# A gated expert block with a quantised feed-forward: the opening and the last expert step in another order on every engine

## The reference

```python
def _L0_xattn_ref(hidden_states, token_ids, Wg, Wu, Wd):     # Wg = Wu = Wd = ctx_2048, 4 experts of 512 x 512
    expert_ids = jnp.minimum(jnp.clip(token_ids, 0, 24999) // 6250, 3)
    for e in range(4):
        g = jax.nn.silu(jnp.einsum('bsd,fd->bsf', hidden_states, Wg[e]))
        u = jnp.einsum('bsd,fd->bsf', hidden_states, Wu[e])
        y = jnp.einsum('bsf,df->bsd', g * u, Wd[e])
        out = jnp.where((expert_ids == e)[..., None], y, out)
def _L0_ffn_ref(x, gate_w, up_w, down_w, ...):               # 512 -> 1536 -> 512, weights rounded to fp8
    gate = jax.nn.silu(_quantized_matmul(x, gate_w, gate_scale))
    up = _quantized_matmul(x, up_w, up_scale)
    return _quantized_matmul(gate * up, down_w, down_scale)
x = x + jnp.tanh(g_xattn[0]) * _L0_xattn_ref(_layernorm(x), itok, ctx_2048, ctx_2048, ctx_2048)
x = x + jnp.tanh(g_ffn[0]) * _L0_ffn_ref(_layernorm(x), gate_w, up_w, down_w, ...)
```

## Time and profile before

| | us |
|---|---|
| median of 3 runs | 406.75 |
| lowest, highest | 406.28, 407.37 |
| the profiled execution's own time | 406.11 |
| its span | 404.4 |
| PE busy | 379.4 (94%) |
| DVE, ACT, POOL busy | 219.1, 187.3, 161.2 |

### The profile page before, as it was taken

How to read it: one execution, slowest core, us unless ns; L and a number is a source line. 1 busy time by engine, 2 the same in 40 slices (tenths; PEclk the granted TensorE clock), 3 DMA queues, 4 the chain that set the end, 5 groups by cost and what they waited for, 6 DMA issues and landing times.

```text
span 404.4 us, 6038 instructions
## 1 busy us (share of the span) xinstructions
PE 379.4 (94%) x1912; PEld 183.2 (45%) x1912; DVE 219.1 (54%) x465; ACT 187.3 (46%) x294; POOL 161.2 (40%) x199
## 2 busy tenths in 40 slices
PE   2889799999999899999999999999999999999990
PEld 2445355545555444444444444444444444444440
DVE  5876888797867786787524222224222225222243
ACT  4777756787886536694432222222222222222220
POOL 2678989997989930411008100006200005300003
PEclk9999999999999999999999999999999999999997
DMA  7697783444445340670002000001100001100002
GB/s 259 167 343 196 138 193 113 68 117 80 105 105 117 94 104 2 151 165 25 0 2 78 28 0 0 2 0 53 52 0 0 0 0 40 66 0 2 0 0 104
DMA packets 40075, 29.99 MB, mean 74 GB/s; under 512 B 31192, under 2 KB 31216, under 8 KB 40048
## 3 DMA queue, kind: packets, MB, share of 16 engines
q1 hardware_dynamic: 37488, 21.26, 22.2%
q0 software_dynamic: 2560, 8.39, 6.1%
HBM read 18.11 MB, written 4.19 MB: 55 GB/s over the span
## 4 chain that ended last, share of the span: by engine, by line
PE 81%; DVE 8%; POOL 3%; issue 3%; ACT 2%; DMA 1%; DVEq 0%; POOLq 0%; ACTq 0%
PE bank L1415 41%; PE bank L1423 20%; PE bank L1314 9%; PE bank L1333 8%; PE bank L1262 2%; POOL xs L502 1%; DVE stats L978 1%; DMA xs<-in_x,order 1%; DVE row_hot L913 1%; ACT xn L676 1%; DVE xs L1243 1%; DVE hTl L995 1%; DVE X L1240 1%; DVE xs L1028 1%; ACT hTh L744 1%
## 5 line engine op out<-in xcount | busy, mean ns | idle before, releaser
L1415 PE MATMUL bank<-X,W 128*128 128x512 f16 (+1 forms) x768 | 173.3, 379 | 0.0
L1415 PEld LDWEIGHTS bank<-X,W 128*128 128x128 bf16 x768 | 75.0, 98 | 90.9 <-ACT late_norms L802 0.5
L1189 DVE SCALAR_TENSOR_TENSOR cs<-bank,up_mul,cs 128x512 f32<-128x512 f32 x48 | 36.0, 751 | 108.7 <-PE bank L1415 104.6
L1423 PE MATMUL bank<-W,cs 128*128 128x512 bf16 x376 | 88.7, 379 | 0.0
L776 ACT ACTIVATE cs<-bank,gate_mul 128x512 f32<-128x512 f32 x48 | 32.9, 686 | 80.0 <-PE bank L1415 80.0
L783 ACT ACTIVATE cs<-cs 128x512 f16<-128x512 f32 x47 | 29.5, 628 | 77.8 <-DVE cs L1189 77.6
L633 POOL TENSOR_TENSOR xs<-xs,X 128x512 f32<-128x512 f32 x12 | 15.3, 1274 | 125.2 <-DVE X L1240 124.9
L1423 PEld LDWEIGHTS bank<-W,cs 128*128 128x128 f16 x376 | 36.5, 98 | 43.7 <-DVE cs L1197 0.2
L1333 PE MATMUL bank<-M,X 128*128 (+1 forms) x228 | 52.3, 379 | 3.1 <-DVE X L999 2.1
L1197 DVE TENSOR_TENSOR cs<-cs 128x512 f16<-128x512 f32 x47 | 33.8, 719 | 31.5 <-ACT cs L783 31.5
L1314 PE MATMUL bank<-M,hTh 128*128 (+1 forms) x152 | 45.1, 378 | 3.2 <-DVE xs L1028 3.2
(11 more groups left out here) (164 smaller groups left out, 379.8 us busy)
## 6 DMA issues: line engine op xcount, KB each, us to landing
ws<-in_L_ffn_gate_w SPq DMA_DIRECT2D x12, 256.0 KB, 2.7
ws<-in_L_ffn_up_w SPq DMA_DIRECT2D x12, 256.0 KB, 2.7
ws<-in_L_ffn_down_w SPq DMA_DIRECT2D x12, 256.0 KB, 2.9
cs<-in_ctx SPq DMA_DIRECT2D x2, 1024.0 KB, 6.6
X<-in_ctx SPq DMA_DIRECT2D x2, 1024.0 KB, 6.9
xs<-in_x,order POOLq DMA_INDIRECT x16, 4.3
dsc<-in_L_ffn_down_scale SPq DMA_DIRECT2D x1, 256.0 KB, 7.0
X<-x2rows SPq DMA_TRANSPOSE x16, 3.1
```

Source lines behind the costliest of these rows:

```text
L1189: v.scalar_tensor_tensor(out=fuse[:, c % 2, :], in0=UP[c % 2][:], scalar=up_mul[:, c:c + 1], in1=sg[:, c % 2, :], op0=ALU.mult, op1=ALU.mu ...
L1415: ins = t_.matmul(dst[c % 2][:].rearrange("p (t i) -> p t i", t=TPG), w, x2_group(g, part, k), start=(k == 0 and part == 0), stop=(k == KC ...
L1423: ins = t_.matmul(ACC[t][:], fuse_part(g, c, part)[:, t * P:(t + 1) * P], W8[:, down_slab(c), :], start=(c == 0 and part == 0), stop=(c == ...
```

## The change

No product is added or left out. What moves:

- **Sort.** The last three of the sixteen `row_hot` blocks are made by POOL (`last_hot`), around its `tile_tok`.
- **Opening on PE.** z of step 0 is cut in two; after its sixth matmul PE turns x of tile 1 into a second bank (`XT` becomes two banks, 2 and 4) and sums the squares for the scales of experts 1 and 2. In steps 1 to 3 the next x is turned ahead of z, from step 4 on behind it as before. The 6 and 4 matmuls that only fill time (on `bank7`) are gone; the 16 ahead of the first turn stay. The three words of the expert walk are loaded before z of step 0. The f32 sum for expert 3 goes from step 1 to step 2.
- **ACT.** Expert 2's squares are cut in two halves; expert 3's squares go from step 0 to step 1; `expert_rows_high` of 1 stays in step 0, that of 2 and the rescaling go to step 2, that of 3 to the head of step 3, and expert 3's rescaling is dropped.
- **POOL.** `step_mask` becomes `mask_places`, `mask_starts`, `mask_last`, laid between the gathers and `ln_scalars`; `y_table` becomes one of 3 steps (experts 0 to 2) before step 0 and one of 16 steps in step 1; expert 3's low part leaves POOL; gathers 9 to 15 are issued later, in steps 0 and 2 to 4.
- **DVE.** `expert_scales(1)`, `step_hot` and the small tables stand elsewhere in step 0, the tables of all experts in step 2; `expert_low(1)` goes from step 0 to step 1; `expert_low(3)` is new on DVE, in step 3; `x1_low` is ahead of `product_h` in steps 0, 1, 3 and 4; `dsb` is made in the feed-forward's first group.
- **Slabs.** Steps with two slabs are 7, 9, 12, 14, 16 instead of 5, 8, 11, 14, 16; slab 0 is rounded at the head of POOL's step 2.
- **Last step.** `h_low(17)` and `add_expert(16)` stand ahead of the chain of small operations `ffn_norms`.

```diff
         def quantised(lo):
-            return 0 if lo < 2 or lo >= STEPS - 1 else 2 if lo in (5, 8, 11, 14, 16) else 1
+            return 0 if lo < 2 or lo >= STEPS - 1 else 2 if lo in (7, 9, 12, 14, 16) else 1
...
             def step(s, lo):                          # POOL
                 if lo >= X2_LAG:
                     x2_low(s - X2_LAG)
+                if lo == 2:
+                    round_slab(0, 0)
                 ln_scalars(s + STATS1_LEAD, lo % 2, 0 if lo + STATS1_LEAD < TILES else 1,
                            2 if lo >= STATS2_LAG else 1)
                 if lo == 0:
-                    y_table()
-                if lo < 2:
-                    expert_low(lo + 2)
-                slabs = slabs_of(s, lo)
+                    gather(9, gathered[5])
+                    expert_low(2)
+                if lo == 1:
+                    y_table(1, E, slice(E - 1, STEPS))
+                slabs = slabs_of(s, lo) if lo != 2 else []
...
             def step(s, lo):                          # ACT
+                if lo < 2 or lo in (3, 4):
+                    x_high(s + 1)
                 if lo < 2:
+                    normalise(s + 2)
+                if lo == 2:
+                    expert_rows_high(2)
+                    normalise(4)
+                    expert_rows_scaled(2)
+                if lo == 3:
+                    expert_rows_high(3)
+                silu(s, lo)
...
             def product_z(s, lo, matrices, operands): # PE
+                pe.wait_ge(m_ready, matrices)
                 pe.wait_ge(xlo_done, min(s + 1, TILES))
                 for n, (lhs, rhs) in enumerate(operands):
+                    if lo == 0 and n == 6:
+                        turn_x(1)
+                        pe.wait_ge(ssq_done, 4)
+                        t_.matmul(SMALL[:, M_SUM + 1:M_SUM + E - 1], ones32[:], part_ssq[:, 1:E - 1], ...)
...
             def step(s, lo):                          # PE
-                product_z(s, lo, z_next[0])
-                if lo < TILES - 1:
-                    pe.wait_ge(xn_done, s + 2)
-                    transpose4(XT, xn, xT_done)
-                if lo == 0:
-                    for i in range(WORDS):
-                        load_word(t_, words, i)
-                    for i in range(6):
-                        t_.matmul(bank[7][:], row_hot[:, 0, :], row_hot[:, 0:KC, :]...)
+                if 1 <= lo < E:
+                    turn_x(s + 1)
+                product_z(s, lo, *z_next[0])
+                if E <= lo < TILES - 1:
+                    turn_x(s + 1)
...
             def step(s, lo):                          # DVE
+                if lo == 3:
+                    expert_low(3)
+                    h_low(s - 1, lo - 1)
+                    add_expert(1)
                 product_h(s, lo)
-                if lo == STEPS - 1:
-                    ffn_norms(SMALL, 0, 2)
...
+                if lo >= 1 and lo != 3:
+                    h_low(s - 1, lo - 1)
+                if lo == STEPS - 1:
+                    norms_in()
+                    add_expert(s - 2)
+                    ffn_norms(0, 2)
```

More of the change, by code:

```diff
@@ L216, in build @@
         order_done = sem("order_done")
-        gathered = [sem(f"gathered{i}") for i in range(7)]
+        gathered = [sem(f"gathered{i}") for i in range(8)]
         mask_done = sem("mask_done")
@@ L514, in ln_scalars, with mask_places @@
                                 ALU.mult).then_inc(ln_done, 1)
[L516 to L528, removed]
             starts = [base[:, e * TILES:e * TILES + 1] for e in range(1, E)]
-            def step_mask():
+            def mask_places():
                 pool.wait_ge(e_of_done, 1)
@@ L570, in expert_low @@
                                     ALU.subtract).then_inc(mlow_pool, 1)
-            step_mask()
-            for t in range(10, 12):
-                gather(t, gathered[5])
+            gather(0, gathered[0])
+            gather(1, gathered[1])
+            gather(2, gathered[1])
+            mask_places()
+            ln_scalars(0, 0, 0, 1)
+            gather(3, gathered[2])
+            mask_starts()
+            ln_scalars(1, 1, 0, 1)
+            gather(4, gathered[3])
+            ln_scalars(2, 2, 0, 1)
+            gather(5, gathered[3])
+            gather(6, gathered[4])
+            ln_scalars(3, 3, 0, 1)
+            gather(7, gathered[4])
+            mask_last()
+            y_table(0, E - 1, slice(0, E - 1))
+            gather(8, gathered[5])
             def round_slab(n, slot):
@@ L680, in x_high @@
                 act.wait_ge(xT_done, tile + 1)
[L681 removed]
+                a.activation(x2_part(tile, 0), XT[tile % 2][:].rearrange("p (k i) -> p k i", k=KC),
                              ACT.Copy).then_inc(xhi_done, 1)
@@ L1126, in step @@
                     aggregate(3, 3, 0, 1)
+                    load_word(v, words, 0)
+                if lo == 1:
+                    expert_low(1)
+                if lo == 2:
+                    round_stats(1, 1)
+                    expert_scales(E - 1, E)
+                    expert_y_scales(1, E - 1, E)
+                    add_expert(0)
+                if lo == 3:
+                    expert_low(3)
+                    h_low(s - 1, lo - 1)
+                    add_expert(1)
+                product_h(s, lo)
@@ L1392, in norms @@
                 ins.then_inc(norm_done, 1)
+            for i in range(WORDS):
+                load_word(t_, words, i)
             z_next = [z_operands(0, 0)]
```

259 lines of the change are left out of this document (147 added, 112 removed).

## The result

| | median us | lowest, highest | executions |
|---|---|---|---|
| before | 407.16 | 406.04, 408.50 | 20 |
| changed | 404.54 | 403.31, 410.45 | 20 |

The ratio is 0.9947 with an interval of 0.9933 to 0.9960, which is 2.2 us; the medians differ by 2.6. I had forecast 4.0 (402.7). So it is faster, by roughly half to two thirds of the forecast; 404.54 lies inside my range (400.9 to 404.9), near its upper end. The profiled execution took 404.58, with a span of 402.8. The two highest times are of disturbed executions and are not in the ratio.

The account below looks back on a forecast made before the run. PE was taken as the bound, busy 379.4 of 404.4 us, with waits and filling left in the opening. Opening 3.6, middle 0 and last step 0.4 sum to 4.0 us, giving a median of 402.7, range 400.9 to 404.9.

Parts of the forecast that it names:

- Opening: PE from the first z to y2: less waiting and filling, gain 3.6 us (4.0 less 0.4), ends 2.2 and 4.3.
- z0 at 18.76: First z on PE: three sort blocks moved to POOL bring its start from 19.32 to 18.76, 0.56 us earlier.
- z2 at 27.5: z of step 2 on PE starts 2.6 us earlier, with `x1_low(2)` ending at 26.9.
- Rest: Small leftovers: walk loads covered by the 1.50 us wait before z0, `dsb` costs nothing, transposes and slab 4's load earlier.
- The collision that I had counted: Opening: DVE's `expert_low(3)` blocks POOL for 2.2 us; with 4.50 taken off it, POOL nets +2.3.
- The 0.4 that I had set aside for steps 4 to 6: Steps 4 to 6: DVE stays some 0.5 us behind, z6 waits for `x1_low(6)`, losing another 0.3 to 0.6.
- Rival A: Opening: DVE's three long expert operations delay PE and meet POOL; opening gives 2.2, end 0, so 404.5 us; chance 0.11.
- Middle: Steps after the opening: POOL's nearly full row keeps up with PE, priced at 0, from -0.4 to +0.4 us.
- Last step: y17 starts 0.86 us earlier, 0.45 is given back before y18; net +0.4, from -0.1 to +0.86.
- Rival C: Opening: the clock falls to 1.2 GHz in PE's waits, one step at that level costs 6.2 us, so 408.9; chance 0.03.
- B: POOL's 21st slab still ends at 138.4, PE waits before y18, all but some 0.5 given back, 406.2 us; chance 0.07.
- D: Sort: POOL's blocks cost 1.1 each or more, sort 0.5 later, 403.8 us; chance 0.77 together with the forecast.

Follow-up runs that it names:

- e3: Changed kernel with all 16 `row_hot` blocks on DVE and none on POOL: 404.99 us.
- e10: Changed kernel with DVE's load of the first walk word put ahead of the scales of experts 1 and 2: 404.07 us.
- e8: Changed kernel with expert 3's low part back on POOL and its rescaling back on ACT, as before: 406.73 us.
- e13: Changed kernel with, in step 10 only, DVE's add of step 8 ahead of that step's statistics: 403.30 us.
- e6: Changed kernel with the old slab counts and slab 4's load issued ahead of the last expert's transposes: 404.37 us.
- e2: Changed kernel with the old slab counts (two in steps 5, 8, 11, 14, 16): 409.80 us.
- e4: Changed kernel with the last step's old order on DVE, small norm chain ahead of `h_low(17)` and `add_expert(16)`: 404.20 us.
- e14: Changed kernel plus early word load, 6 fillings before z0, early slab 4 load, step 8's add first in step 10, add of 17 ahead of feed-forward scales: 402.49.

## Why the prediction was right in direction and wrong in size

- **Opening, forecast 3.6, measured 2.67 (z5).** The order of events was right, and y1's wait of 2.47 is gone as forecast. Two terms failed.
  - *z0 at 18.76, measured 19.29.* I took 0.56 for the sort and carried all of it to z0. `order` gained 0.37, and z0 was 0.03 to 0.2 earlier, since an idle of 0.36 is new ahead of DVE's preparation. From z0 to z5 are 30.2 us in seven traces with z0 between 19.17 and 19.31, so these 0.53 arrive at z5 in full. e3 shows that three blocks on POOL gave their 0.5 all the same: without them z0 is at 19.72.
  - *z2 at 27.5, measured 28.59.* I laid the order down by durations alone and left out the walk's word that DVE loads ahead of `product_h(0)`, priced under "Rest" as covered, which was true of PE's loads and not of DVE's. It stands as 0.76 of idle DVE:

```profile
25.45 0.75 DVE L1151 SCALAR_TENSOR_TENSOR h<-bank,h_scale,silu_z 128x512 f32<-128x512 f32 x1 [0.76 <-issue]
```

  e10 shows 0.96 between z1 and z2, of which 0.38 is left at z5.
  - y2 was late by 1.31; 0.53 and 0.38 of it are these two. For the other 0.4 DVE's row is the place, since it works without a pause from 37.15 to the end of `product_h(3)` at 46.36, for which PE waits 0.60. The collision that I had counted, DVE's `expert_low(3)` over POOL's table, costs DVE nothing (2.50, where `expert_low(1)` takes 2.48 before; POOL's table took 1.30 and 1.11 where e8 has 0.29 and 0.24, and PE doesn't wait for it). The one that I hadn't counted goes the other way. Under POOL's `expert_low(2)`, from 36.63 on, DVE's tables of step 2 took 0.57 and 1.19, and `w_big` 0.79; before they took 0.23, 0.21 and 0.43, together 1.7 less. That this makes the 0.4 is read from the trace and no run tests it. First the changed kernel, then before:

```profile
38.91 1.19 DVE L1063 TENSOR_TENSOR step_sel<-step_hot,h_scale 128x64 f32<-128x64 f32 x1
...
36.63 4.51 POOL L583 TENSOR_TENSOR W<-X,W 128x512 f16<-128x512 f32 x4 [1.63 <-ACT X L704]
...
34.01 0.21 DVE L1013 TENSOR_TENSOR step_sel<-step_hot,h_scale 128x64 f32<-128x64 f32 x1
```

  - The 0.4 that I had set aside for steps 4 to 6 was not needed: from y2 to z5 are 2.59 us before and after. That is luck: 1.31 less 0.4 are the 0.9 that the opening missed.
- **Rival A (DVE's debt) gives the right number for other reasons.** Its 404.5 is the measured median, and its 2.2 for the opening is near. But its three long pieces on DVE were no longer than before (`expert_scales(1)` 1.33, the low parts 2.47 and 2.50), and e8 shows that the alternative to `expert_low(3)` on DVE costs 2.2.
- **Middle, forecast 0, measured -0.76** (2.67 at z5, 1.91 at z18). It is one wait of 0.96 that comes or not by chance; without it the middle gains 0.2, and in e13's trace it takes 79.55 where before takes 79.89. My bounds of 0.4 had no room for a collision on the path. POOL's first rounding came at 45.11, not at 43.8, and its 21st slab ended at 136.5. The counts of slabs don't matter there (e6), but POOL's row isn't free: with 4.5 us more on it the kernel is 2.2 slower (e8).
- **Slabs.** I put the new counts down to POOL's time where the gathers stand. e2 and e6 show that they keep clear of slab 4's landing; without them the changed kernel would have been slower than before, at 409.8. This is a rival that I hadn't seen. Under "Rest" I wrote that the transposes end and slab 4 is loaded earlier; it is issued 3.1 later (before, then changed), while ACT in e2 asks for it at 55.0 and before at 57.85:

```profile
54.94 11.28 SPq L428 DMA_DIRECT2D ws<-in_L_ffn_up_w  x4
...
58.08 7.64 SPq L431 DMA_DIRECT2D ws<-in_L_ffn_up_w  x4
```

- **Last step, forecast +0.4, measured -0.3.** y17 is 0.92 earlier relative to z18 (7.28 for 8.20), as forecast (0.86). The term that was mis-sized is what is given back: 0.45 taken, 1.2 measured, and y18's wait of 1.04 is over the microsecond that I had named as a sign of being wrong. The add of 17 started 6.35 after y17 and ended at 7.1, where my chain ended at 5.95 to 6.95, since f_scale (1.12, before 0.26) and the rounding (1.67) both met POOL; I had let only the rounding meet it:

```profile
140.16 1.12 DVE L1112 TENSOR_SCALAR f_scale<-f_top 128x8 int32<-128x8 int32 x1 [0.30 <-POOL f_top L619]
...
142.19 1.67 DVE L1244 SCALAR_TENSOR_TENSOR W<-w_big,w_sum 128x512 bf16<-128x512 f32 x1
143.78 0.74 DVE L1078 SCALAR_TENSOR_TENSOR xs<-bank,y_step,xs 128x512 f32 x1
```

- **Rival C (the clock).** I had it as a whole step at the lower level and at 0.03. It exists at a quarter to a third of that price, 1.4 to 1.9, in some executions. It may not be new: before has executions with a mean clock of 0.987 that are about 1 us longer, but no trace of one.
- **Rivals B and D** fell: POOL isn't waited for before y18, and its blocks at 0.65 to 0.85 are dear and still worth it.

The sum in the traces: 2.67 - 0.76 - 0.31 = 1.6, which is 404.4 less 402.8. The medians differ by 2.6, since the profiled execution of before (406.11) was 1.05 under its median and the changed kernel's lay at its median. What makes most executions of before longer than that one isn't shown.

## What to carry to other kernels

When DVE and POOL both run back to back, look for pairs that start within a tenth of a microsecond of each other and ask what stands behind the one that may come second: put the operation that TensorE waits for ahead of the pair, even where it looks idle. Read scatter between executions as a list of such places: two groups 0.7 to 0.9 apart went with one wait of 0.96, and moving one add ahead of a few small operations removed both the wait and the scatter. And when work is pulled forward, follow its input's transfer back to the queue it stands in, since a load behind an unrelated landing is late without any engine being slow.

## What was not expected of the hardware

- A collision of DVE and POOL is decided by who comes first, at distances of 0.02 to 0.05 us, and cost the second 0.25 to 1.0. A DVE table of 64 columns went from 0.21 to 1.19.
- The clock fell to its lower level for 3.4 us after waits of 0.84 to 0.98 and some 1.7 us in four traces, and not in eight where the first wait was 0.67 or less. It also fell behind the waits of 3.25 (e2) and 2.79 (e4).
- A word loaded by DVE between two of its instructions cost 0.76 us of its time, and nothing in the place where it waits anyway: z1 starts at 24.10 in e14 and at 24.15 in the changed kernel.
- Transposes in the DMA queues vary between traces: the load behind the last four was issued at 58.08 in the changed kernel's and at 62.58 in that of e4, whose edit lies far behind this place.
